# Building the edge counts of three types in one sweep

## The reference

```python
h = maximum(layernorm(x), 0)
msg_t = relu(h[src] @ W_e[t].T + b_e[t])               # t = 0, 1, 2
S_t   = segment_sum(where(edge_type == t, msg_t, 0), dst)
agg   = concat([relu(h), S_0, S_1, S_2])               # 512 wide
upd   = agg @ W_n[node_type].T + b_n[node_type]
out   = x + upd + h
```

## Time and profile before

| | |
|---|---|
| timed runs, median (lowest to highest) | 1322.74 us (1322.64 to 1323.84) |
| profiled execution, first to last instruction | 1595.0 us |
| granted TensorE clock in it, mean | 0.927 |
| PE busy | 1392.9 us, 87% |
| DVE busy | 1114.8 us, 70% |
| ACT busy | 584.8 us, 37% |
| POOL busy | 920.6 us, 58% |
| moved by DMA | 120.60 MB, mean 76 GB/s |

### The profile page before, as it was taken

One profiled execution on the slowest core, in us unless ns is written; L12 is line 12 of the kernel. 1 busy time (PEld: TensorE's weight loads), 2 busy tenths in 40 slices (PEclk: granted clock), 3 DMA queues, 4 the chain that ended last, 5 costly groups with the idle time before them and its releaser, 6 DMA issues.

```text
span 1595.0 us, 26681 instructions
## 1 busy us (share of the span) xinstructions
PE 1392.9 (87%) x9175; PEld 946.5 (59%) x9175; DVE 1114.8 (70%) x3845; ACT 584.8 (37%) x1165; POOL 920.6 (58%) x979
## 2 busy tenths in 40 slices
PE   7867998998999988898989888988797898888898
PEld 3544665666666656566666566656565565655565
DVE  8786887777878786777777676865565566555542
ACT  6753443433443433343334333432232223222220
POOL 3376666665666665655665565665555565555552
PEclk9978999998999999999999899999998899888989
DMA  9652222122222531222222223321211121111211
GB/s 283 215 136 54 74 72 78 49 74 72 77 50 61 170 88 47 76 60 57 76 79 58 54 65 110 101 54 50 55 45 50 50 52 49 50 47 49 54 46 37
DMA packets 97259, 120.60 MB, mean 76 GB/s; under 512 B 19947, under 2 KB 77170, under 8 KB 97124
## 3 DMA queue, kind: packets, MB, share of 16 engines
q0 software_dynamic: 29568, 60.61, 15.2%
q1 hardware_dynamic: 67078, 58.03, 11.8%
q10 hardware_dynamic: 478, 0.23, 0.0%
HBM read 93.12 MB, written 25.68 MB: 74 GB/s over the span
## 4 chain that ended last, share of the span: by engine, by line
PE 78%; another core or an unknown queue 6%; issue 6%; DVE 6%; ACT 3%; SPq 1%; DMA 0%; DVEq 0%; ACTq 0%
PE ps L807 33%; PE ps L791 23%; PE ps L770 12%; PE ps L829 6%; ACT arena L957 2%; PE ps L826 2%; DVE arena L1216 1%; DVE lhot L1230 1%; PE ps L707 1%; PE ps L814 1%; PE ps L825 1%; DMA acc<-in_dst_dram 0%; DVE work L1323 0%; DVE stats L1088 0%
## 5 line engine op out<-in xcount | busy, mean ns | idle before, releaser
L647 POOL DMA_INDIRECT rows<-message_table,idx x924 | 893.9, 967 | 601.8 <-PE ps L770 239.9
L957 ACT CAST arena<-ps 128x490 f16<-128x490 f32 (+2 forms) x966 | 495.5, 566 | 924.3 <-PE ps L791 585.0
L807 PE MATMUL ps<-mem,arena 128*128 128x384 bf16 x3381 | 659.1, 339 | 12.7 <-DVE mem L1328 6.4
L1216 DVE TENSOR_SCALAR arena<-iota_j,jkey 128x441 bf16<-128x441 f16 (+3 forms) x1794 | 465.8, 324 | 182.8 <-PE ps L791 113.8
L791 PE MATMUL ps<-arena,lhot 128*128 128x294 bf16 (+8 forms) x2622 | 398.2, 284 | 155.4 <-ACT arena L957 78.8
L807 PEld LDWEIGHTS ps<-mem,arena 128*128 128x128 f16 x3381 | 333.6, 103 | 225.8 <-issue 48.0
L791 PEld LDWEIGHTS ps<-arena,lhot 128*128 128x128 bf16 x2622 | 218.8, 102 | 270.7 <-issue 137.8
L1230 DVE TENSOR_TENSOR lhot<-ps,lkey 128x512 bf16<-128x512 f32 (+1 forms) x412 | 297.2, 721 | 0.0
L1297 DVE TENSOR_TENSOR acc<-ps,acc 128x60 f32 (+1 forms) x369 | 80.3, 218 | 267.7 <-PE ps L770 138.0
L770 PEld LDWEIGHTS ps<-onehot,rows 128*128 128x128 f32 x1848 | 250.1, 205 | 18.0 <-issue 8.1
L770 PE MATMUL ps<-onehot,rows 128*128 128x27 f32 x1848 | 244.1, 274 | 4.6 <-DVE acc L1297 4.0
(11 more groups left out here) (129 smaller groups left out, 412.6 us busy)
## 6 DMA issues: line engine op xcount, KB each, us to landing
rows<-message_table,idx POOLq DMA_INDIRECT x924
work<-message_table SPq DMA_DIRECT2D x21, 448.0 KB
kept_planes<-work SPq DMA_DIRECT2D x14, 672.0 KB
mem<-kept_planes SPq DMA_DIRECT2D x14, 672.0 KB
message_table<-work SPq DMA_DIRECT2D x25, 192.0 KB, 2.1
message_table<-rows SPq DMA_DIRECT2D x24, 192.0 KB, 2.0
own_hT<-work SPq DMA_DIRECT2D x49, 64.0 KB, 1.8
work<-own_hT SPq DMA_DIRECT2D x49, 64.0 KB
```

The lines of the kernel that those rows point to most:

```text
L647: pool.indirect_dma_start(out=rows[:, s % SLOTS, u, :], out_offset=None, in_=table_rows, in_offset=bass.IndirectOffsetOnAxis(ap=idx[:, gro ...
L807: m = pe.matmul(psQ[q % 2][0:BW * SL, 0:3 * D], counts[q % 2][:, c * MC + e, :], planes[:, c * MC + e, :, :].rearrange("p v d -> p (v d)") ...
L957: act.copy(counts[q % 2][:, :, a:a + n], psB[m % 3][:, 0:HB * n].rearrange("p (w h) -> p h w", w=n)).then_inc(d_count, 1)
L1216: dve.tensor_scalar(to, iota_j[:, 0:HB * D_WID[u]], float(t * JT), jkey[:, w, u:u + 1], ALU.add, ALU.is_equal)
```

## The change

The dense way builds one matrix of counts for all three types. A column mask carries 1, 16 or 256 by the edge's type instead of 1 for one type (`wkey`), so that a count matrix holds three fields: bits 0 to 3, 4 to 7 and 8 to 10 of a 16-bit integer. ACT evicts it as int16. A new DVE step, `digits`, cuts one field out of seven blocks of it with a bitwise AND (128 x 896) into one of four slots (two in the first steps). PE reads the slot as 16-bit floats: the cut bits, read so, are the count times a power of two, which the DVE adds multiply out later (`add_scaled`).

- 26 batches instead of 23 take the last 99,840 edges, so 208 gather groups are left of 231. LEAD grows to 12, the gather slots shrink to 5. There are 78 pairs, with types innermost, so 546 product pieces, and 52 windows built once.
- The planes of all three types stay in SBUF. All 21 chunks are loaded and split at the start, the first three before step 0 and then two a step (`SPLIT`). Storing, fetching and the later splitting are gone. A product of the first batch may not be dealt before two steps after its chunk.
- A column of ones is added to the planes. It counts the edges that a product has seen; the total (`seen`) decides, with the old flag, whether the last branch recomputes everything.
- The node sums of 49 blocks in `acc` are replaced by two rings of 6 blocks, one for each way. `shift` moves them along, 5 times for the gathers and 6 times for the windows. `finish` reads both rings where a block lies under both.
- The memory of the table phase lies in `mem` now, so the raw loads wait for the last transpose of that phase. The scratch for descriptors of POOL's DMAs is 4096 bytes a partition instead of the default.

```diff
-BATCHES = 23
+BATCHES = 26
...
-LEAD = 2
-SLOTS = 6
+LEAD = 12
+SLOTS = 5
...
+UNIT = 2.0 ** 24
+LANE = (1.0, 16.0, 256.0)
+FIELD = (0x00F, 0x0F0, 0x700)
+DIGS = 4
+RING_S = 6
+RING_D = 6
...
-    for q in range(1, NQ):
-        for k in range(BG):
-            DENSE += [("build", q * BG + k), ("prod", (q - 1) * MC + k)]
-        DENSE += [("prod", (q - 1) * MC + c) for c in range(BG, MC)]
-    DENSE += [("prod", (NQ - 1) * MC + c) for c in range(MC)]
+    for b in range(BATCHES):
+        for k in range(BP):
+            if b + 1 < BATCHES and k % 3 == 0 and k // 3 < BG:
+                DENSE.append(("build", (b + 1) * BG + k // 3))
+            DENSE.append(("prod", b * BP + k))
+
+    SPLIT = (-1, -1, -1, 0, 0, 1, 1, 2, 2, 3, 3, 4, 4, 5, 5, 6, 6, 7, 7, 8, 8)
...
-            while z < len(DENSE) and (room >= size(DENSE[z]) / 2 or s == D1):
+            while (z < len(DENSE) and (room >= size(DENSE[z]) / 2 or s == D1)
+                   and not (DENSE[z][0] == "prod" and DENSE[z][1] < BP and s < SPLIT[DENSE[z][1]] + 2)):
...
+    SWITCH = min(p for p in range(NQ * MC) if PROD_STEP[p] >= SPLIT[-1] + 3)
+
+    def slot_of(p):
+        return p % 2 if p < SWITCH else p % DIGS
...
-        acc = sb("acc", [P, T, NA])
...
-        mem = sb("mem", [P, NB * 3 * D // 2])
+        ring_s = sb("ring_s", [P, T, LEFT + RING_S * P])
+        ring_d = sb("ring_d", [P, T, RING_D * P])
...
+        mem = sb("mem", [P, T * NB * PW // 2])
...
             def load_planes(m):
-                if m >= 3:
-                    sp.wait_ge(m_low, m - 2)
...
+                if m >= MC:
+                    sp.wait_ge(m_top, m - MC + 1)
...
-            def load_raw(k):
...
-            def keep(k):
...
-            def fetch(k):
...
+            sp.wait_ge(turn_t, TYP + 1)
+            for m in range(BP):
                 load_planes(m)
+            sp.wait_ge(m_low, BP)
...
             def product(i):
                 q, c = divmod(i, MC)
...
+                pe.wait_ge(dig_ok, i + 1)
                 for e in range(MC):
-                    m = pe.matmul(psQ[q % 2][0:BW * SL, 0:3 * D], counts[q % 2][:, c * MC + e, :],
-                                  planes[:, c * MC + e, :, :].rearrange("p v d -> p (v d)"), start=(c + e == 0),
+                    m = pe.matmul(psQ[q % 2][0:BW * SL, 0:3 * D + 1], dig_f[:, slot_of(i), e, :],
+                                  planes[:, t, c * MC + e, 0:3 * D + 1], start=(c + e == 0),
...
                 def column_hot(to, u):
-                    dve.tensor_scalar(to, iota_j[:, 0:HB * D_WID[u]], float(t * JT), jkey[:, w, u:u + 1],
-                                      ALU.add, ALU.is_equal)
+                    dve.tensor_scalar(to, iota_j[:, 0:HB * D_WID[u]], jkey[:, w, u:u + 1], wkey[:, w, u:u + 1],
+                                      ALU.is_equal, ALU.mult)
...
+            def shift(one, move, step, count):
+                steps_, (a, n) = move[2], move[3]
+                dve.wait_ge(fin_mm, finished(step))
+                for k, (was, now) in enumerate(steps_):
+                    dve.wait_ge(acc_add, count - len(steps_) - 1 + k)
+                    dve.tensor_copy(one[:, :, now * P:(now + 1) * P], one[:, :, was * P:(was + 1) * P]).then_inc(acc_add, 1)
...
+            def digits(p):
+                q, c = divmod(p, MC)
+                b, t = divmod(q, T)
+                if p % BP == 0:
+                    dve.wait_ge(d_count, BW * PIECES * (b + 1))
+                if SLOT_USER[p] is not None:
+                    dve.wait_ge(d_prod, SLOT_USER[p] + 1)
...
+                dve.tensor_scalar(dig[:, slot_of(p), :, :], counts[b % 2][:, c * MC:(c + 1) * MC, :], FIELD[t], None,
+                                  ALU.bitwise_and).then_inc(dig_ok, 1)
...
+                dve.tensor_scalar(seen[:, q:q + 1], psQ[q % 2][0:BW * SL, 3 * D:3 * D + 1], UNIT / LANE[q % T], None, ALU.mult)
```

More of the change, by code:

```diff
@@ L8 @@
 F16 = mybir.dt.float16
+I16 = mybir.dt.int16
 ALU = mybir.AluOpType
@@ L82, in build @@
     NQ = T * BATCHES
-    NA = LEFT + NB * P + SL
     NP = D // P + T
+    PW = 3 * D + 2
+    BP = T * MC
     SB_ = 2
@@ L150, in plan @@
         last = [at[q * MC + MC - 1] for q in range(NQ)]
-        wide_done = [last[NQ - BATCHES + w // BW] + 2 for w in range(NW)]
+        wide_done = [last[w // BW * T + T - 1] + 2 for w in range(NW)]
         ready = [max([s for s in range(NS) if touches(group_at(s), i)] + [wide_done[w] for w in range(NW) if wide_touches(w, i)])
@@ L187, in build, with places @@
         THROUGH.append(n)
+    def places(j):
+        i, step, out, wait = ORDER[j], FIN[j] + 1, [], THROUGH[READY[ORDER[j]]]
+        moved = [(kind, k) for s, kind, k in MOVED_AT if s <= step]
+        if any(touches(g, i) for g in range(NS)):
+            out.append(("s", i - BASE_S[min(step, NS - 1)]))
+        if any(wide_touches(w, i) for w in range(NW)):
+            out.append(("d", i - BASE_D[max(b for b in range(BATCHES) if b == 0 or LAST[b * T] + 2 <= step)]))
+        return out, max([wait] + [MOVED[m] for m in moved])
     def sums_of(s):
@@ L390, in build @@
         acc_add = sem("acc_add")
-        m_in = [sem(f"m_in{i}") for i in range(3)]
+        m_in = [sem(f"m_in{i}") for i in range(MC)]
         m_top = sem("m_top")
@@ L839, in _ @@
                     finish(j)
-                for kind, i in pieces(s)[:1]:
-                    if kind == "build":
-                        count(i)
-                    else:
-                        product(i)
-                for kind, i in pieces(s)[1:]:
+                for kind, i in pieces(s)[:2]:
                     if kind == "build":
@@ L851, in _ @@
                     turn_slots(q)
+                for kind, i in pieces(s)[2:]:
+                    if kind == "build":
+                        count(i)
+                    else:
+                        product(i)
+                if s == CHECK + 1:
+                    pe.wait_ge(d_count, BATCHES * BW * PIECES)
+                    pe.wait_ge(seen_in, 1)
+                    pe.matmul(psB[0][0:1, 0:P], seen_all[:, 0:1], ident[:, :], start=True, stop=True).then_inc(seen_t, 1)
+            pe.wait_ge(ctl_ok, 1)
             rest = pe.value_load(flag[0:1, 0:1], min_val=0, max_val=1)
@@ L1297, in add_to, with add_scaled @@
                 dve.tensor_tensor(there, sums_, there, ALU.add).then_inc(acc_add, 1)
+            def add_scaled(there, sums_, scale, count):
+                if count > 1:
+                    dve.wait_ge(acc_add, count - 1)
+                dve.scalar_tensor_tensor(out=there, in0=sums_, scalar=scale, in1=there,
+                                         op0=ALU.mult, op1=ALU.add).then_inc(acc_add, 1)
+            def shift(one, move, step, count):
[4 more added lines that the diff above has]
+                    dve.tensor_copy(one[:, :, now * P:(now + 1) * P], one[:, :, was * P:(was + 1) * P]).then_inc(acc_add, 1)
+                dve.wait_ge(acc_add, count - 1)
+                dve.memset(one[:, :, a * P:(a + n) * P], 0.0).then_inc(acc_add, 1)
             def add(s):
@@ new lines, in all_seen, with judge @@
+            def all_seen():
+                dve.wait_ge(d_sum, NQ)
+                link(dve.tensor_reduce(seen_all[:, :], seen[:, :], AX_X, ALU.add))
+                dve.sem_inc(seen_in, 1)
+            def judge():
+                dve.wait_ge(seen_t, 1)
+                link(dve.tensor_reduce(seen_ok[:, 0:1], psB[0][0:1, 0:P], AX_X, ALU.add))
+                link(dve.scalar_tensor_tensor(out=seen_ok[:, 1:2], in0=seen_ok[:, 0:1], scalar=float(NW * WE),
+                                              in1=rest_row[:, :], op0=ALU.is_equal, op1=ALU.mult))
+                dve.tensor_scalar(flag[:, 0:1], seen_ok[:, 1:2], -1.0, 1.0, ALU.mult, ALU.add).then_inc(ctl_ok, 1)
```

409 lines of the change are left out of this document (219 added, 190 removed).

## The result

The changed kernel takes **1225.75 us** (median of 3 runs, 1224.01 to 1226.79) where the kernel before takes 1322.74: a ratio of 0.927, 95% interval 0.925 to 0.9289. The forecast was 1210, its range 1175 to 1300. The profiled execution spans 1224.0 us with a mean clock of 0.977, so here the trace can be set against the median directly.

The account below looks back on a forecast made before the run. The prediction took PE to bound the kernel, with POOL close behind. From 1322.7 us it took 144 less PE work, added 26 for the start and 5 for ring moves: 1210 us, own range 1185 to 1240, stated range 1175 to 1300.

Parts of the forecast that it names:

- New PE work of 1062 us: PE's builds, products, gathers, node blocks and transposes at full clock: 1062 us in all, 144 less than before.
- the ring moves: 11 moves of about 3 us on DVE, only partly inside its cover: +5 us (0 to 20).
- The first build starts at 77.98: Start of PE's main work in the kernel before, added to 1206 us of PE work to account for 1284.
- The start, 26 us: Steps 0 to 9: DVE's chunk splitting sets 6.9 us a step and PE idles; 26 us more, bounds +7 and +46.
- at POOL's pace of 5 us a step: Lower bound for the start: POOL sets the steps, PE idles 12 us, so +7.
- Cuts at 0.40: Each of 546 field cuts on DVE takes 0.40 us, 218 us in all.
- The cover of 1.3 us a step: Main part: DVE needs 3.7 us before the first new cut, PE has 5.0, so the wait is priced at nothing.
- 1: Rival: POOL becomes the bound, cuts delaying its DMAs; 1281 us, or 1229 with a quarter of the delay; chance 0.10.
- 2: Rival: the cut runs at one element a cycle, 1.03 us, making DVE 5.1 a step; 1299 us; chance 0.06.
- 3: Rival: with cuts at 1.03 us, cuts chain DVE and PE at 6.5 us a step; 1447 us, slower; chance 0.06.
- 4: Rival: PE takes fields with zero exponent bits as zero, so the last branch recomputes everything; 50 ms; chance 0.02.
- 5: Rival: nothing lost in the start, and PE's old waits shrink as DVE empties; 1170 us; chance 0.04.

Follow-up runs that it names:

- x_loads: Changed kernel with five of SP's 22 edge loads moved to ACT's queue, on a halting chip: 1387.97 us, beside 1389.05 for the unaltered changed kernel.
- x_pitch392: Changed kernel with the planes of a node block 784 bytes apart instead of 772: 1219.54 us, ratio 0.9227 to the kernel before.
- x_nosplit: Changed kernel with 18 of 21 chunks not split by DVE, zeros written for the low plane, on a halting chip: 1377.81 us.
- y_nosplit: Repeat of x_nosplit beside the unaltered changed kernel, on a halting chip: 1376.06 us, against 1389.05 for the unaltered one.
- x_cut2: Changed kernel with each of the 546 field cuts done twice, first into an unread buffer: 1246.73 us, ratio 0.9425 to the kernel before.
- x_cut3: Changed kernel with each field cut done three times, with a wait between: 1355.69 us, ratio 1.0263 to the kernel before.

## Why the prediction was right

**The sum held where its terms came from the trace.** New PE work of 1062 us was the main term. PE is full, 993 us busy in 1000, and steps 10 to 200 take 5.36 us each for the 5.24 reckoned, which bears the term out within 3%. The forecast was 15.75 us short; two terms give 15, but the ring moves, charged 5, gave nothing, so 5 us have no named cause. PE's 7.6 us of waits for DVE after 190 us are of that size; no run separates them.

- *"The first build starts at 77.98"* was carried over unchanged. It starts at 85.24 now: **7.3 us**, and the first gather at 84.32 for 78.30. "Its first gather waits for the table either way" was true and beside the point, since the table is late. The change raises LEAD from 2 to 12 and the windows from 46 to 52, so the far edges are read as 64 rows for 48, into DMA engines that are full; SP's first store of the table moves from 15.81 to 21.17. That more rows on full DMA engines are the cause is argued from these rows, and the engines were as full before; x_loads excludes only the issuing. The prediction looked at the diff of the loop and not at what one constant does 80 us earlier.
- *Products at 1.14 a piece, 163 ns each*: 165.0 in the mean, 3822 x 2 = **8 us**, of which the pitch is 6 by x_pitch392.

**The start, 26 us**, came out in size: the first ten steps take 6.82 us each, forecast 6.9, DVE full from 112 us on, PE at half clock in 95:112. x_nosplit and y_nosplit bear the mechanism out in part only: without splitting the steps take 5.9 to 6.2, where "at POOL's pace of 5 us a step" was the other bound. DVE's work fills the steps as reckoned, but taking it away frees less than the reckoning says. What holds the steps then is not known.

**Cuts at 0.40** measure 0.412. The Trainium skill (VectorE: DVE Perf Modes, The perf-mode tier table) gave 233 ns of streaming as an estimate and did not name the bitwise form; with the 200 ns that the mask rows leave at no elements (345 - 441 x 0.33) that is 0.43, and the row agrees. A cut also starts its successor after 302 ns, too soon for half that rate (467 ns, the estimate doubled). "The slope of the mask rows agrees with the four" was read too kindly: 0.33 ns an element, where 233 ns over 896 elements are 0.26.

**DVE** was put at 802 us and is 869. The term that was too small is the masks, 2.23 us a build: a new mask takes 407 ns for 345 at 441 elements, and 357 for 297 at 294. It has two pointer operands for one and other operations, and no run separates these. 780 masks x 60 ns are 47 us of the 67, all in DVE's idle. The cover of 1.3 us a step was therefore nearer to 1.1. x_cut2, which adds 171 / 208 = 0.8 a step in the mean, already shows some waits, since the steps are not equal.

**The ring moves, 5**, were 0 within the error; **ACT** hides (the eviction's idle is PE's, 815.0 of 823.4).

**The rivals.** 1, POOL: its mean of 1011 missed the test of "under 1.0 us", yet three quarters of its work gives the same time, so it does not set the pace; on a halting chip, which the prediction did not consider, it does take part. 2 and 3: the cut is not 1.03 us, and if it were, x_cut2 and x_cut3 put the time near 1350, between the two, with no full chain. 4: the last branch, at 50 ms, is not run, so the counting column reaches its number and fields with all exponent bits zero are multiplied as they stand. 5: the start did lose what was said.

## What to carry to other kernels

Sum the engine that is full from start-to-start distances, but read the start of the program as its own stage: what is late there, as the table is here, moves everything behind it. When an operand's pitch changes, look at its alignment before its length. And price a new instruction on the second-busiest engine by doing it twice and three times: the two runs give both its room and its slope. Read what was added from the engine's busy time, since durations that overlap add up to more. And before two profiles are compared, see that they are of one kind.

## What was not expected of the hardware

- One program takes 1226 or 1389 us, and another 1321 or 1592, by the chip it runs on (or the moment). On the longer ones PE's instructions come one to three at a time for some microseconds, with 61.6 us of idle for which the trace shows no wait, while POOL at first goes on; its own "remote" waits number 75. It happens with four indirect DMAs a step and hardly with three (0.8 us). How far POOL runs ahead does not matter.
- Matmuls of 384 or 385 bf16 columns stand at two levels, 162 and 166 ns, when their rows start at multiples of 772 bytes, and at one, 163, with 784. With 385 columns the lower level belongs to the rows a multiple of 16 bytes from the first.
- A 16-bit mask on VectorE takes 60 ns more with two pointer operands, is_equal and mult, than with one, an immediate, add and is_equal (407 for 345 at 441 elements).
- A bitwise AND of 128x896 int16 takes 412 ns, and the next instruction starts after 302.
